# A grouped whitening kernel: partition rows reordered to (channel, sample), a round of 24 slots in place of 28, Gram pieces in halves and products of 392 columns

## The chip, the cores and the metric

One NeuronCore of one Trainium2 chip runs the whole kernel. The metric is the device time of one execution, in microseconds (us). Everything is float32.

## The reference

The input x is 32 samples by 128 channels by 56x56 pixels (3136). Four neighbouring channels of one sample are normalised together (group norm with 32 groups), and the result is whitened in 16 groups of 8 channels: the 8x8 covariance over all samples and pixels, its inverse square root, one product.

```python
def _gn(v, G=32, eps=1e-05):
    g = v.reshape(B_, G, C_ // G, H_, W_)
    m = jnp.mean(g, axis=(2, 3, 4), keepdims=True)
    s = jnp.var(g, axis=(2, 3, 4), keepdims=True)
    return ((g - m) / jnp.sqrt(s + eps)).reshape(v.shape)

def _zca_forward(x, weight, bias, groups=16):       # c = 8 channels, M = 32 * 3136
    xf = jnp.transpose(x, (1, 0, 2, 3)).reshape(C, M)
    xc = xf - jnp.mean(xf, axis=1, keepdims=True)
    xg = xc.reshape(G, c, M)
    cov = jnp.einsum('gim,gjm->gij', xg, xg) / M + 1e-4 * jnp.eye(c)
    e, v = jnp.linalg.eigh(cov)
    proj = jnp.einsum('gik,gk,gjk->gij', v, jax.lax.rsqrt(e), v)
    xw = jnp.einsum('gij,gjm->gim', proj, xg).reshape(C, M)
    return (xw * weight + bias)                     # back to (N, C, H, W)

x = x + _zca_forward(_gn(x), L0_conv_weight, L0_conv_bias)
```

## The kernel before

**Tiles.** A channel group (8 channels, g = 0 to 15) is two tiles, s = 0 and 1. A tile has 128 partition rows, 16 samples by 8 channels, and 3136 pixels in the free dimension: 1.6 MB. It is loaded into one of 13 places of `ring`, normalised in place, and overwritten with the output before it is stored. So 51.4 MB come in and 51.4 MB go out. In the kernel before, row p is sample p // 8, channel p % 8.

**What a group needs, in order.**
- Four loads per tile, each of 32 rows (4 samples by 8 channels), issued by GpSimd (`load`): `x_dram[g, s, q]`, with q = 0 and 2 in one pair and 1 and 3 in the next. They are issued two groups ahead of use.
- VectorE: 14 `row_stats` (448 columns each), then `stats_rows`, `stats_mean`, `stats_var`, `stats_reciprocal`, `stats_heron`, `stats_scale`, with two small averaging products on TensorE (`mean_average`, `var_average`) and a root on ScalarE between them. The last of them gives `y_mul` and `y_add`.
- GpSimd: `normalise`, 8 pieces of 784 columns, with the loads and small operations between them.
- VectorE: `turn`, 8 transposes in 32x32 blocks, of 13, 12, 12 and 12 units of 64 columns per tile, into a ring of three `y_t`. A turn needs the normalised columns that it covers; the first one of a tile covers 832 and so needs two pieces.
- TensorE: `gram`, one product of 64x64 per unit, added up in `ps_gram`. A float32 product is two MATMUL instructions, so a turn is 24 or 26 of them.
- VectorE: `gram_masked_blocks` and `gram_sum` read `ps_gram`; the first Gram product of the next group waits until the former has read it (`gram_masked`).
- The solve: 20 hops (`HOPS`), tiny products on TensorE, each of which needs what ScalarE or VectorE read of the one before: MU, COV, then 15 that alternate between two products read by ScalarE (`HOP_YUZ`) and one read by VectorE (`HOP_M`), then T, V and ROOT. VectorE makes of ROOT the 128x128 matrices `a_mat`, one for each tile.
- TensorE: `apply`, 14 products of 128x128 by 448 columns; ScalarE: `finish`, 8 evictions of two banks or one (896 or 448 columns) that add the shift and write the output into `ring`.
- SyncE: `store`, two DMAs per tile, of 64 rows each (8 samples by 8 channels), issued when the tile's last eviction is done. The last tile of all is stored in two parts.

**The order of the work.** It is written out by hand. Every engine runs the same loop over rounds i and over slots j of a round (`SLOTS`, 28). Each operation of a group has a slot number counted from the group's own round (`HOP_AT`, `APPLY_AT`, `TURN_AT`, `STAT_DVE_AT` and so on); a number of 28 or more falls into a later round. So in one round TensorE works on the Gram products of one group, on the solve of that group and the one before, and on the apply products of an older one, and VectorE gathers the statistics of the next group. Engines run strictly in their program's order, and semaphores make them wait for each other; within a slot TensorE's order is hop, averaging product, apply, Gram piece, and VectorE's is hop, `gram_masked_blocks`, turn, statistics, `row_stats`.

## Time and profile before

| | |
|---|---|
| time, median of 3 runs | 548.48 us (542.95 to 552.39) |
| time of the profiled execution | 546.78 us |
| its span, first to last instruction | 545.2 us |
| mean granted TensorE clock | 0.946 |
| TensorE busy | 420.7 us (77%) |
| VectorE busy | 318.2 us (58%) |
| GpSimd busy | 217.1 us (40%) |
| ScalarE busy | 154.3 us (28%) |
| DMA | 104.04 MB, mean 191 GB/s |

Busy shares are means over a span that has a start without products and an end without anything but stores, so they say little about which engine a round waits for. TensorE's small products overlap in the records: a product's modelled end lies up to 0.08 us behind the start of the next one. The profiled execution's time is its span and 1.6 us around it.

### The profile page before, as it was taken

How to read it: one execution, taken by the hardware profiler on the slowest of the kernel's cores; microseconds unless marked ns; L12 is line 12 of the kernel's file. 1: busy time of each engine (PE TensorE's matmuls, PEld its weight loads, DVE VectorE, ACT ScalarE, POOL GpSimd, SP SyncE). 2: the span in 40 equal slices, each digit the busy share in tenths (PEclk: the TensorE clock that was granted, in tenths of full speed). 3: DMA queues.
4: the chain of work that ended last, by engine and by line, in shares of the span. 5: the costliest groups of instructions: out<-in, count | busy, mean ns of one | idle time of the engine just before them, and what ended most of it. 6: DMA issues, size and time to landing. Idle time of an engine off the chain costs nothing.

```text
span 545.2 us, 11695 instructions
## 1 busy us (share of the span) xinstructions
PE 420.7 (77%) x4708; PEld 244.2 (45%) x4708; DVE 318.2 (58%) x853; ACT 154.3 (28%) x353; POOL 217.1 (40%) x324
## 2 busy tenths in 40 slices
PE   0036688888888989888988989898989888898820
PEld 0025554454455545444454545454554545553310
DVE  0668676767567676767576666766676766431100
ACT  0000013333233233332233323333333233333520
POOL 6054908172453627090815445361809060600000
PEclk9998569999899999999799999999999999999975
DMA  7965434757485857576575848485767634444443
GB/s 168 223 167 187 120 120 121 251 170 272 159 277 175 248 203 243 209 226 221 185 249 149 285 172 280 177 250 199 233 218 218 241 113 105 120 111 128 139 174 129
DMA packets 23652, 104.04 MB, mean 191 GB/s; under 512 B 15152, under 2 KB 15152, under 8 KB 15536
## 3 DMA queue, kind: packets, MB, share of 16 engines
q0 software_dynamic: 18432, 51.44, 30.6%
q1 hardware_dynamic: 5168, 51.87, 29.7%
q8 instruction: 38, 0.62, 0.5%
q14 instruction: 14, 0.11, 0.1%
HBM read 51.86 MB, written 51.38 MB: 189 GB/s over the span
## 4 chain that ended last, share of the span: by engine, by line
PE 55%; DMA 13%; DVE 11%; issue 7%; POOL 7%; ACT 3%; DVEq 0%; ACTq 0%; POOLq 0%
PE ps_apply L540 28%; DMA ring<-in_x_dram 13%; PE ps_gram L540 13%; PE ps_small L540 12%; POOL ring L294 3%; DVE bn L340 3%; POOL ring L288 3%; DVE y_t L389 3%; PE ps_stat L540 2%; ACT st L498 1%; DVE mv L346 1%; DVE a_mat L435 1%; DVE pp L417 1%; DVE pb L430 1%; ACT zx L498 1%
## 5 line engine op out<-in xcount | busy, mean ns | idle before, releaser
L294 POOL TENSOR_SCALAR ring<-ring,y_mul,y_add 128x784 f32<-128x784 f32 x128 | 126.6, 993 | 255.1 <-DVE y_add L379 253.4
L540 PE MATMUL ps_apply<-ring,a_mat 128*128 128x448 f32 x448 | 227.5, 594 | 0.6 <-ACT ring L492 0.3
L340 DVE BATCH_NORM_STATS2 bn<-ring 128x6 f32<-128x448 f32 x224 | 132.7, 598 | 22.5 <-DMA ring<-in_x_dram 22.4
L540 PEld LDWEIGHTS ps_gram<-y_t 128*64 128x64 f32 x3136 | 111.1, 146 | 59.8 <-issue 37.1
L492 ACT ACTIVATE ring<-ps_apply,fin_add 128x896 f32<-128x896 f32 (+1 forms) x128 | 115.7, 906 | 76.8 <-PE ps_apply L540 76.8
L540 PE MATMUL ps_gram<-y_t 128*64 128x64 f32 x3136 | 129.2, 235 | 8.9 <-DVE y_t L389 8.9
L389 DVE STREAM_TRANSPOSE y_t<-ring 128x768 f32<-128x768 f32 (+1 forms) x128 | 125.8, 984 | 16.1 <-POOL ring L294 16.1
L288 POOL DMA_DIRECT2D ring<-in_x_dram x128 | 75.9, 594 | 2.4 <-issue 1.4
L540 PEld LDWEIGHTS ps_apply<-ring,a_mat 128*128 128x128 f32 x448 | 68.6, 190 | 13.9 <-ACT ring L492 3.6
L417 DVE SCALAR_TENSOR_TENSOR pp<-ps_small,cst 16x16 f32<-16x16 f32 x112 | 17.5, 156 | 88.8 <-PE ps_small L540 88.2
L498 ACT COPY st<-ps_small 16x32 f32<-16x32 f32 (+1 forms) x128 | 22.2, 174 | 155.3 <-PE ps_small L540 155.3
L540 PEld LDWEIGHTS ps_small<-pp,st 16*16 16x16 f32 x224 | 12.4, 89 | 55.6 <-issue 53.5
L540 PE MATMUL ps_small<-st 16*16 16x16 f32 x224 | 23.0, 176 | 18.2 <-ACT st L498 18.2
L540 PEld LDWEIGHTS ps_small<-st 16*16 16x16 f32 x224 | 12.7, 89 | 44.4 <-issue 42.2
L540 PE MATMUL ps_small<-pp,st 16*16 16x16 f32 x224 | 23.2, 177 | 10.3 <-DVE pp L417 8.5
L540 PE MATMUL ps_small<-st,pp 16*16 16x16 f32 x256 | 25.2, 172 | 5.5 <-DVE pp L417 5.5
L540 PE MATMUL ps_stat<-mv,cst 128*128 128x2 f32 x32 | 6.5, 273 | 21.9 <-DVE mv L346 21.9
L540 PEld LDWEIGHTS ps_small<-st,pp 16*16 16x16 f32 x256 | 14.7, 89 | 6.7 <-issue 6.7
L540 PEld LDWEIGHTS ps_stat<-mv,cst 128*128 128x128 f32 x32 | 5.2, 203 | 24.2 <-DVE mv L346 13.9
L393 DVE TENSOR_TENSOR g_masked<-ps_gram,cst 128x64 f32<-128x64 f32 x16 | 3.6, 225 | 20.3 <-PE ps_gram L540 20.3
L498 ACT COPY mu<-ps_small 128x32 f32<-128x32 f32 x16 | 3.0, 186 | 43.0 <-PE ps_small L540 43.0
L498 ACT COPY zx<-ps_small 8x128 f32<-8x128 f32 x16 | 4.1, 255 | 36.1 <-DVE res L422 36.1
(59 smaller groups left out, 192.9 us busy)
## 6 DMA issues: line engine op xcount, KB each, us to landing
ring<-in_x_dram POOLq DMA_DIRECT2D x128, 392.0 KB, 8.2
out_dram<-ring SPq DMA_DIRECT2D x62, 784.0 KB
out_dram<-ring SPq DMA_DIRECT2D x2, 448.0 KB
out_dram<-ring SPq DMA_DIRECT2D x2, 336.0 KB
cst<-const_dram SPq DMA_DIRECT2D x1, 472.0 KB
wb<-in_L_conv_weight_dram SPq DMA_DIRECT2D x1, 0.5 KB
wb<-in_L_conv_bias_dram SPq DMA_DIRECT2D x1, 0.5 KB
```

What stands on the lines that cost most here:

```text
L288: pool.dma_start(ring[32 * q:32 * (q + 1), slot(g, s), :], x_dram[g, s, q]).then_inc(x_landed[slot(g, s)], 16)
L294: nc.gpsimd.tensor_scalar(y, y, y_mul[:, g, s:s + 1], y_add[:, g, s:s + 1], ALU.mult, ALU.add).then_inc(y_ready, 1)
L340: nc.vector.bn_stats(bn[:, g % 2, s, b, :], ring[:, slot(g, s), b * BN:(b + 1) * BN]).then_inc(bn_done, 1)
L346: nc.vector.bn_aggr(mv[:, g, s, :], bn[:, g % 2, s].rearrange("p b k -> p (b k)")).then_inc(stat_step, 1)
L389: nc.vector.transpose(y_t[:, n % TURN_RING, 0:hi - lo], ring[:, slot(g, s), lo:hi]).then_inc(turned, 1)
L393: nc.vector.tensor_tensor(g_masked[:], ps_gram[:, 0:UNIT], k_("gmask"), ALU.mult).then_inc(gram_masked, 1)
L417: nc.vector.scalar_tensor_tensor(out=pp[:], in0=s_m, scalar=POLY[it][1], in1=ai[:, 2 * CG * it:2 * CG * (it + 1)], op0=ALU.mult, op1=ALU.a ...
L430: nc.vector.tensor_tensor(by_sample(pb[:]), spread, by_sample(w_mask[:, g % 2]), ALU.mult).then_inc(tail_step, 1)
L435: nc.vector.scalar_tensor_tensor(out=a_mat[:, g % 2, s], in0=k_("ident"), scalar=scale[:, g, s:s + 1], in1=pb[:], op0=ALU.mult, op1=ALU.ad ...
L492: nc.scalar.activation(dst, ps_apply[:, bank:bank + chunks, 0:APPLY], ACT.Identity, bias=fin_add[:, g, s:s + 1], scale=1.0).then_inc(out_r ...
L498: nc.scalar.copy(dst, src).then_inc(solve_read, 1)
L540: return nc.tensor.matmul(out_, lhsT, rhs, start=start, stop=stop, skip_group_check=True)
```

## The change

- **Rows.** A tile's rows are now four bands of 32, and within a band row = channel * 4 + sample. The loads and the stores take their view of DRAM as (channel, sample) for each band: a load's outermost dimension is 8 channels where it was 4 samples; a store is four DMAs of 32 rows (8 channels by 4 samples) where it was two of 64 rows (8 samples by 8 channels). Masks and the views that spread a small matrix over samples follow (`by_sample`, `for_samples`), with one dimension more.
- **Slots.** A round has 24 slots where it had 28. The hops from the third on stand in successive slots (18 hops in 18 slots; before, 9 slots for 8 hops). A turn comes every third slot as before, its Gram products are split in two parts in the two slots that follow (6 units, then 6 or 7). The other slots take the apply products.
- **Products.** 16 apply products of 392 columns replace 14 of 448; each is evicted by itself (16 evictions of 392 columns where there were 8), two slots after it is issued, over four banks.
- **Statistics.** `row_stats` stand in two slots of three and end earlier; the averaging product of the mean is in slot 22 of the round before and that of the variance in slot 0; `stats_scale` is in slot 4 as before, the first turn in slot 6 where it was in slot 7.
- **Small.** The MU hop has one more product (a constant 128x128 by `neg_mean`, 2 columns), from which `fin_add` is made. Every tile is stored whole, the last too.

All the new names that depend on `BLOCKS` have their values for `BLOCKS = 1`: loops over it run once.

```diff
-APPLY = 448
-APPLY_TILE = HW // APPLY
-APPLY_CHUNKS = TILES * APPLY_TILE
-PIECE_CHUNKS = ((2, 2, 2, 1), (2, 2, 2, 1))
-PIECE_TILE = len(PIECE_CHUNKS[0])
-PIECES = TILES * PIECE_TILE
-CHUNK_PIECE = [(PIECE_TILE * s + k, b) for s in range(TILES) for k, n in enumerate(PIECE_CHUNKS[s]) for b in range(n)]
-PIECE_LAST = [max(c for c, (p, _) in enumerate(CHUNK_PIECE) if p == k) for k in range(PIECES)]
-SLOTS = 28
+BLOCKS = 1
+BLOCK = P // BLOCKS
+STRETCH = HW // BLOCKS
+APPLY = 392
+ROUND_TILE = STRETCH // APPLY
+ROUNDS = TILES * ROUND_TILE
+BANK_SETS = 4 // BLOCKS
+ROWS_OF = 4
+BANDS = P // (ROWS_OF * CG)
+STORED = 16 * BLOCKS * BANDS
+SLOTS = 24
...
-BN_AT = [2 * b for b in range(TILES * BN_CHUNKS)]
-STAT_DVE_AT = [28, 29, 30, 31, 31, 32]
-STAT_PE_AT = [28, 30]
-ROOT_AT = 31
-TURN_AT = [7 + 3 * b for b in range(TURNS)]
-GRAM_LAG = 2
-GRAM_READ_AT = TURN_AT[-1] + GRAM_LAG + 1
-HOP_AT = [GRAM_READ_AT, GRAM_READ_AT + 1] + [GRAM_READ_AT + 2 + (9 * k) // 8 for k in range(HOPS - 2)]
-APPLY_AT = [HOP_AT[-1] + 2 + 2 * c for c in range(APPLY_CHUNKS)]
-FINISH_LAG = 1
+BN_AT = [3 * (b // 2) + b % 2 + 1 for b in range(TILES * BN_CHUNKS)]
+STAT_DVE_AT = [BN_AT[-1] + 1 + k for k in (0, 2, 4, 6, 6, 7)]
+STAT_PE_AT = [BN_AT[-1] + 2, BN_AT[-1] + 4]
+ROOT_AT = BN_AT[-1] + 6
+TURN_AT = [6 + 3 * b for b in range(TURNS)]
+GRAM_AT = [a + 2 + h for a in TURN_AT for h in range(2)]
+GRAM_READ_AT = GRAM_AT[-1] + 1
+HOP_AT = [GRAM_READ_AT, GRAM_READ_AT + 2] + [GRAM_READ_AT + 3 + k for k in range(HOPS - 2)]
+FIRST_APPLY = next(a for a in range(HOP_AT[-1] + 2, HOP_AT[-1] + 5) if a % 3 == 1)
+APPLY_AT = [FIRST_APPLY + SLOTS * c // ROUNDS for c in range(ROUNDS)]
+FINISH_LAG = 2
...
-        x_dram = x.rearrange("(s q n) (g c) h w -> g s q n c (h w)", s=TILES, q=4, c=CG)
-        out_dram = out.rearrange("(s a n) (g c) h w -> g s a n c (h w)", s=TILES, a=2, c=CG)
+        x_dram = x.rearrange("(s q n) (g c) h w -> g s q c n (h w)", s=TILES, q=BANDS, c=CG)
+        out_dram = out.rearrange("(s q n) (g c) h w -> g s q c n (h w)", s=TILES, q=BANDS, c=CG)
...
         def by_sample(a):
-            return a.rearrange("p (n c) -> p n c", c=CG)
+            return a.rearrange("p (q c n) -> p q c n", c=CG, n=ROWS_OF)
+        def for_samples(a):
+            return a.unsqueeze(1).unsqueeze(3).broadcast_to([P, BLOCK // (ROWS_OF * CG), CG, ROWS_OF])
...
         def _(sp):
             def store(g, s, lo, hi):
-                px = slice(lo, hi)
-                for a in range(2):
-                    rows = slice(a * HALF, (a + 1) * HALF)
-                    sp.dma_start(out_dram[g, s, a, :, :, px],
-                                 ring[rows, slot(g, s), px]).then_inc(out_stored[slot(g, s)], 16)
+                for r in range(BLOCKS):
+                    for q in range(BANDS):
+                        k, band = divmod(q, BANDS // BLOCKS)
+                        px = slice(k * STRETCH + lo * APPLY, k * STRETCH + hi * APPLY)
+                        at = slice(r * STRETCH + lo * APPLY, r * STRETCH + hi * APPLY)
+                        sp.dma_start(out_dram[g, s, r * (BANDS // BLOCKS) + band, :, :, px],
+                                     ring[32 * q:32 * (q + 1), slot(g, s), at]).then_inc(out_stored[slot(g, s)], 16)
             sp.dma_start(cst[:], const).then_inc(const_landed, 16)
             with nc.allow_non_contiguous_dma(reason="256 channel scalars, once"):
                 sp.dma_start(wb8[:, 0, :], weight.rearrange("(g j) o -> j (g o)", j=CG)).then_inc(const_landed, 16)
...
-            for g in range(GROUPS - 1):
-                for s in range(TILES):
-                    sp.wait_ge(out_ready, PIECES * g + PIECE_TILE * (s + 1))
-                    store(g, s, 0, HW)
-            g = GROUPS - 1
-            sp.wait_ge(out_ready, PIECES * g + PIECE_TILE)
-            store(g, 0, 0, HW)
-            sp.wait_ge(out_ready, PIECES * g + PIECE_TILE + 2)
-            store(g, 1, 0, 4 * APPLY)
-            sp.wait_ge(out_ready, PIECES * (g + 1))
-            store(g, 1, 4 * APPLY, HW)
+            for n in range(TILES * GROUPS):
+                g, s = divmod(n, TILES)
+                sp.wait_ge(out_ready, BLOCKS * ROUND_TILE * (n + 1))
+                store(g, s, 0, ROUND_TILE)
             for n in range(TILES * GROUPS - RING, TILES * GROUPS):
-                extra = 32 if n == TILES * GROUPS - 1 else 0
-                sp.wait_ge(out_stored[n % RING], 32 * (n // RING + 1) + extra)
+                sp.wait_ge(out_stored[n % RING], STORED * (n // RING + 1))
...
-                nc.vector.tensor_reduce(g_pad[:, CG:2 * CG], g_masked[:].rearrange("p (n c) -> p c n", c=CG),
-                                        AX.X, ALU.add).then_inc(gram_reduced, 1)
+                nc.vector.tensor_reduce(g_pad[:, CG:2 * CG], g_masked[:].rearrange("p (q c n) -> p c q n", c=CG, n=ROWS_OF),
+                                        AX.XY, ALU.add).then_inc(gram_reduced, 1)
...
-            def finish(g, k):
-                s, b = divmod(k, PIECE_TILE)
-                if k == 0:
+            def finish(g, c):
+                s, h = divmod(c, ROUND_TILE)
+                n = ROUNDS * g + c
+                if c == 0:
                     act.wait_ge(shift_step, 2 * (g + 1))
-                chunks = PIECE_CHUNKS[s][b]
-                hi = (PIECE_LAST[k] + 1 - APPLY_TILE * s) * APPLY
-                act.wait_ge(applied, APPLY_CHUNKS * g + PIECE_LAST[k] + 1)
-                dst = ring[:, slot(g, s), hi - chunks * APPLY:hi].rearrange("p (b c) -> p b c", c=APPLY)
-                bank = 2 * (k % 2)
-                nc.scalar.activation(dst, ps_apply[:, bank:bank + chunks, 0:APPLY], ACT.Identity,
-                                     bias=fin_add[:, g, s:s + 1], scale=1.0).then_inc(out_ready, 1)
+                act.wait_ge(applied, n + 1)
+                for r in range(BLOCKS):
+                    at = r * STRETCH + h * APPLY
+                    nc.scalar.activation(ring[:, slot(g, s), at:at + APPLY],
+                                         ps_apply[:, BLOCKS * (n % BANK_SETS) + r, 0:APPLY], ACT.Identity,
+                                         bias=fin_add[:, g % 2, r, s:s + 1], scale=1.0).then_inc(out_ready, 1)
...
-                        act.wait_ge(tail_step, TAIL_OPS * g)
-                    copy(mu[:], s_mu)
+                        act.wait_ge(shift_step, 2 * g)
+                    copy(mu[:], ps_small[:, 0:32 + TILES * BLOCKS])
...
-                nc.scalar.activation(fin_add[:, g], neg_mean[:, g], ACT.Identity, bias=shift[:],
-                                     scale=-1.0).then_inc(shift_step, 1)
+                nc.scalar.activation(fin_add[:, g % 2].rearrange("p r s -> p (r s)"), mu[:, 4 * CG:], ACT.Identity,
+                                     bias=shift[:], scale=-1.0).then_inc(shift_step, 1)
...
-            def gram(g, t):
+            def gram(g, k):
+                t, part = divmod(k, 2)
                 b = t % TURN_TILE
                 n = TURNS * g + t
-                pe.wait_ge(turned, n + 1)
-                if t == 0 and g > 0:
+                if part == 0:
+                    pe.wait_ge(turned, n + 1)
+                if k == 0 and g > 0:
                     pe.wait_ge(gram_masked, g)
-                for u in range(TURN_UNITS[b]):
+                for u in range(6 * part, TURN_UNITS[b] if part else 6):
                     half = ps_gram[UNIT * (u % 2):UNIT * (u % 2 + 1), 0:UNIT]
                     unit = y_t[:, n % TURN_RING, u * UNIT:(u + 1) * UNIT]
                     ins = product(half, unit, unit, start=t == 0 and u < 2,
                                   stop=t == TURNS - 1 and u >= TURN_UNITS[b] - 2)
-                ins.then_inc(gram_done, 1)
+                if part == 1:
+                    ins.then_inc(gram_done, 1)
             def apply(g, c):
-                s, b = divmod(c, APPLY_TILE)
-                k, place = CHUNK_PIECE[c]
+                s, h = divmod(c, ROUND_TILE)
+                n = ROUNDS * g + c
                 if c == 0:
                     wait_apart(pe, tail_step, TAIL_OPS * g + 4)
-                n = PIECES * g + k
-                if place == 0 and n >= 2:
-                    pe.wait_ge(out_ready, n - 1)
-                product(ps_apply[:, 2 * (k % 2) + place, 0:APPLY], a_mat[:, g % 2, s],
-                        ring[:, slot(g, s), b * APPLY:(b + 1) * APPLY]).then_inc(applied, 1)
+                if n >= BANK_SETS:
+                    pe.wait_ge(out_ready, BLOCKS * (n - BANK_SETS + 1))
+                for k in range(BLOCKS):
+                    for r in range(BLOCKS):
+                        rows, at = slice(r * BLOCK, (r + 1) * BLOCK), k * STRETCH + h * APPLY
+                        ins = product(ps_apply[k * BLOCK:(k + 1) * BLOCK, BLOCKS * (n % BANK_SETS) + r, 0:APPLY],
+                                      a_mat[rows, g % 2, s], ring[rows, slot(g, s), at:at + APPLY])
+                ins.then_inc(applied, 1)
...
+                    for r in range(BLOCKS):
+                        product(s_dup[:, r * TILES:(r + 1) * TILES], k_("dup")[:, r * P:(r + 1) * P], neg_mean[:, g])
...
-                    for t, back in due([a + GRAM_LAG for a in TURN_AT], j):
+                    for t, back in due(GRAM_AT, j):
```

Worked out from the new lists, the slots of a round hold on TensorE, in this order (a hop by its number of the 20): slot 7 hop 0 (MU), apply; 8 apply, Gram; 9 hop 1 (COV), Gram; 10 hop 2, apply; 11 hop 3, apply, Gram; 12 hop 4, Gram; 13 hop 5, apply; 14 hop 6, apply, Gram; 15 hop 7, Gram; and so on in threes to slot 21 hop 13, Gram; 22 hop 14, mean product, apply; 23 hop 15, apply, Gram; 0 hop 16, variance product, Gram; 1 hop 17 (T), apply; 2 hop 18 (V), apply, Gram; 3 hop 19 (ROOT), Gram; 4 apply; 5 apply, Gram; 6 Gram.

## Rows read from the trace of the kernel before

**Rows 1.** Windows of rounds: start:end, length, busy (instructions), clock, DMA share, GB/s.
```profile
172.69:201.62 28.93, 25.35 (x296) 14.46 (x295) 19.80 (x54) 9.55 (x22) 13.55 (x21) 1.00 0.68 222
112.69:143.75 31.06, 27.11 (x296) 15.26 (x295) 19.87 (x54) 9.54 (x22) 13.56 (x20) 0.95 0.65 220
260.41:291.89 31.48, 28.00 (x296) 15.79 (x295) 19.93 (x54) 9.55 (x22) 13.56 (x21) 0.89 0.64 202
```

**Rows 2.** Timeline of GpSimd: first normalisation of groups 0, 2 and 15 (start, duration).
```profile
33.12 0.99 POOL L294 TENSOR_SCALAR ring<-ring,y_mul,y_add 128x784 f32<-128x784 f32 x1 [22.47 <-DVE y_add L379]
...
83.73 0.99 POOL L294 TENSOR_SCALAR ring<-ring,y_mul,y_add 128x784 f32<-128x784 f32 x1 [14.60 <-DVE y_add L379]
...
465.90 1.00 POOL L294 TENSOR_SCALAR ring<-ring,y_mul,y_add 128x784 f32<-128x784 f32 x1 [19.97 <-DVE y_add L379]
```

**Rows 3.** Timeline of TensorE in one round; brackets: idle before, and its releaser.
```profile
200.66 1.02 PE L540 MATMUL ps_apply<-ring,a_mat 128*128 128x448 f32 x2
201.61 0.21 PE L540 MATMUL ps_small<-pp,st 16*16 16x16 f32 x2
...
202.23 0.20 PE L540 MATMUL ps_small<-st 16*16 16x16 f32 x2 [0.35 <-ACT st L498]
...
209.08 0.92 PE L540 MATMUL ps_gram<-y_t 128*64 128x64 f32 x24
209.93 0.21 PE L540 MATMUL ps_small<-pp,st 16*16 16x16 f32 x2
...
220.35 0.38 PE L540 MATMUL ps_small<-res,zx 8*128 8x8 f32 x2 [0.53 <-ACT zx L498]
...
225.14 0.38 PE L540 MATMUL ps_stat<-mv,cst 128*128 128x2 f32 x2 [0.81 <-DVE mv L346]
225.38 1.00 PE L540 MATMUL ps_apply<-ring,a_mat 128*128 128x448 f32 x2
```

**Rows 4.** Timeline of VectorE: steps around the solve's last hop and the turns.
```profile
31.89 0.15 DVE L366 RECIPROCAL rec<-root 128x2 f32<-128x2 f32 x1
...
115.01 1.05 DVE L389 STREAM_TRANSPOSE y_t<-ring 128x832 f32<-128x832 f32 x1 [0.77 <-POOL ring L294]
...
220.77 0.29 DVE L430 TENSOR_TENSOR pb<-ps_small,w_mask 128x128 f32<-128x128 f32 x1 [0.76 <-PE ps_small L540]
...
221.77 0.62 DVE L340 BATCH_NORM_STATS2 bn<-ring 128x6 f32<-128x448 f32 x1
...
223.70 0.96 DVE L389 STREAM_TRANSPOSE y_t<-ring 128x768 f32<-128x768 f32 x1
224.58 0.51 DVE L346 BATCH_NORM_AGGREGATE mv<-bn 128x2 f32<-128x42 f32 x2
...
228.40 0.23 DVE L393 TENSOR_TENSOR g_masked<-ps_gram,cst 128x64 f32<-128x64 f32 x1 [1.02 <-PE ps_gram L540]
```

**Rows 5.** Timeline of VectorE: waits for loads.
```profile
29.54 0.63 DVE L340 BATCH_NORM_STATS2 bn<-ring 128x6 f32<-128x448 f32 x1 [2.77 <-DMA ring<-in_x_dram]
...
136.76 0.63 DVE L340 BATCH_NORM_STATS2 bn<-ring 128x6 f32<-128x448 f32 x1 [0.60 <-DMA ring<-in_x_dram]
```

**Rows 6.** Timeline of TensorE: its wait behind the second of these.
```profile
137.88 0.38 PE L540 MATMUL ps_stat<-var,cst 128*128 128x2 f32 x2 [0.42 <-DVE var L354]
```

**Rows 7.** Timeline of ScalarE: the last two evictions of the kernel.
```profile
520.65 1.53 ACT L492 ACTIVATE ring<-ps_apply,fin_add 128x896 f32<-128x896 f32 x2 [0.50 <-PE ps_apply L540]
```

**Rows 8.** Windows: loads alone twice, the fastest microsecond, stores alone twice.
```profile
6.50:34.00 27.50, 2.57 (x8) 2.00 (x8) 12.29 (x35) 0.20 (x1) 5.03 (x9) 1.00 1.01 226
39.00:40.00 1.00, 1.00 (x24) 1.00 (x20) 1.00 (x3) 0.00 (x0) 1.00 (x3) 1.00 0.53 201
213.00:214.00 1.00, 0.65 (x8) 0.35 (x7) 0.56 (x2) 0.00 (x0) 1.00 (x2) 1.00 0.94 389
486.00:500.00 14.00, 12.19 (x126) 6.65 (x126) 3.43 (x14) 5.43 (x12) 0.00 (x0) 1.00 0.42 112
524.00:540.00 16.00, 0.00 (x0) 0.00 (x0) 0.00 (x0) 0.00 (x0) 0.00 (x0) 0.50 0.48 188
```

56 lines of the change are left out of this document (30 added, 26 removed).

## The prediction

> **What bounds the kernel now.** I read the windows of whole rounds first [rows 1]. From the first normalisation of one group to that of the next an ordinary round takes 28.93 us; TensorE is recorded busy for 25.35 of it, VectorE for 19.8, GpSimd 13.55, ScalarE 9.55. So a round is TensorE's program plus its waits. The timeline of GpSimd [rows 2] cuts the span of 545.2 us in four: 33.1 us until group 0 is normalised for the first time; 50.6 us for the first two rounds, which hold few or no apply products; 382.2 us for 13 full rounds (13 x 28.93 would be 376.1, so 6.1 us are extra); 79.3 us after the last group's start.
>
> TensorE's timeline [rows 3] says what the waits are: a hop of the solve that comes behind nothing but its predecessor. The two products at 201.61 are short, yet the next hop starts 0.62 us later, for ScalarE's read and the semaphores; where a Gram piece or an apply product lies between, there is no wait. A round holds seven such waits of 0.35 to 0.53 us and one of 0.81 for `stats_rows` [rows 3]. The recorded idle time is 28.93 - 25.35 = 3.6 us; each wait is really some 0.08 us longer, because a product's recorded end lies behind the start of the next (200.66 + 1.02 against 201.61). With eight waits that is 4.2 us, and 24.7 us of work.
>
> The extra 6.1 us sit mainly in two rounds of 31.06 and 31.48 us, whose granted clock was 0.95 and 0.89 [rows 1]: in each the clock fell from 2.4 to 1.2 GHz. The first fall came after TensorE had waited 0.81 us for the mean and then 0.42 us behind VectorE [rows 6], which itself waited for a load [rows 5]. A round with a fall cost 2.1 and 2.5 us, some 0.5 of the first being the wait.
>
> The ends are bound by DMA. VectorE waits for the third tile until 29.54 [rows 5] and group 0 starts 3.6 us later. The last eviction ends at 522.2 [rows 7], the span 23.0 us after it; in between only stores run [rows 8].
>
> **The change: work of a round.** An apply product of 448 columns takes 0.95 us start to start (200.66 to 201.61), a product of 2 columns 0.24 (225.14 to 225.38) [rows 3]; on that line one of 392 takes 0.86. Sixteen are 13.8 us for 13.3: +0.5 (bounds: 0, if time goes with the columns, and +1.9, if it goes with the instructions). MU's added product is of 2 columns: +0.24. The Gram instructions are the same (24 in 0.85 us); halving them adds eight seams, taken at nothing, up to +0.5. So 24.7 + 0.7 = 25.4 us. The evictions are 16 of 392 columns; ScalarE rises from 9.55 to about 11.5 us of the round, hidden, because four banks give each eviction some four slots.
>
> **The change: waits of a round.** With a hop in each slot every hop from the third to T, V and ROOT has at least half a Gram piece (0.42 us) behind it, and its own issue, some 0.12 for a product (0.20 less the overlap of 0.08) and more for two. That is 0.54 to 0.61 against the 0.62 that passed between 201.61 and 202.23: the seven waits go, but for less than 0.1 each, which I take at nothing. What is late next I follow in VectorE's program, which is strictly in order. Let T be the start of hop ROOT.
> - VectorE reads ROOT at T + 0.42 and is free at T + 1.42 (220.35, 220.77, 221.77) [rows 3, 4]. Then stands the eighth turn (0.88, from 223.70 to 224.58), then `stats_reciprocal`, from which to GpSimd's first piece 1.23 us pass (31.89 to 33.12) [rows 2, 4]: T + 3.5. The first turn needs two pieces, 2.3 us after GpSimd's start (112.69 to 115.01) [rows 1, 4], and takes 0.97; behind it on VectorE stands `gram_masked_blocks` (0.23), for which the first Gram piece waits: T + 7.1.  TensorE needs only 0.32 + 0.42 + 1.72 (two apply) + 0.85 + 0.53 (MU with its new product) + 1.72 = 5.6 us to get there. A new wait of 1.5 us in every round; behind it in TensorE's order stand COV and so the whole solve.
> - VectorE reads COV only behind two `row_stats`: 0.3 us.
> - `stats_rows` stands in slot 21 behind hop 13's read and a turn: it is done 0.24 + 0.1 + 0.88 + 0.56 = 1.8 us after that hop's start; TensorE is there after 0.13 + 0.54 + 0.19. A wait of 0.9, like the 0.81 that it has now [rows 3].
>
> Together 2.7 us, and the round is 25.4 + 2.7 = 28.1, 0.8 less than 28.93. A seventh fewer slots thus gives only 3% of a round: the hops' waits are gone, one of VectorE's and GpSimd's chain has come.
>
> **The change: the clock.** TensorE stands 1.5 us in one place of every round, with the small products of COV behind it, where the 1.23 us (0.81 + 0.42) before the first fall came in two parts. None of the rounds with 0.81 alone had a fall. I therefore expect a fall in some eight of 13 rounds, between none and all, at 2.0 us (the two observed, less the wait in the first): +16.
>
> **The change: transfers.** One pair of loads alone moved 201 GB/s with a DMA share of 0.53: half of the 16 engines, four for each DMA, as many as its outermost dimension (4 samples) [rows 8]. Stores, whose outermost dimension is 8, run at 0.42 and 0.48. With all loads queued in the opening the share is 1.01 and the rate only 226 GB/s: 14 GB/s for each engine, which elsewhere moves 24. So something other than the engines is shared; in one microsecond 389 GB/s were reached. Stores alone likewise run at 112 GB/s and at 188 with the same share. The new layout gives every DMA 8 channels outermost and 32 rows, 4 for each of 8 engines. No row shows a DMA of the new shape. I take 330 GB/s for the opening (bounds 226, no gain, and 389; nearer to the latter, since a pair alone already gives each engine its full 24) and 190 for stores (the 188 without company; bounds 112 and half of 389 at 0.94, which is 207).
>
> The Trainium skill, page SBUF — State Buffer, section Door 1: The DMA port swizzle, says that partitions reach 16 ports in blocks of four and that 0 to 31 and 32 to 63 share eight of them. 
>
> In us: three tiles (4.8 MB) at 330 land by 6.5 + 14.6 = 21.1 for 29.5; VectorE's statistics are then the later, and group 0 starts at about 25: -8 (bounds 0 and -9.5). At the end the last two tiles are evicted 6 us apart; each is stored in 8.5 us at 190 GB/s, so the last, now whole, has its data out 11 us after the last eviction, and with 2 for latency and SyncE's issues the span ends 13 after it, for 23.0: -10 (at 112 GB/s it would be +2). In the rounds no load is late any more.
>
> **The sum**, on the profiled execution's 546.8: opening -8; first two rounds, four slots shorter each and with fewer bare hops, -5 (estimate, 0 to -7); 13 rounds 13 x 28.1 = 365.3 for 382.2, -16.9; clock +16; from the last group's start to the last eviction 56.3 us now, slot 4 to slot 79 in place of 80, but with an emptier TensorE and 16 products: +3 (estimate, 0 to +5); stores -10. That gives 525.9. The median of the runs is 0.3% above the profiled one, within what I can tell: 526.
>
> **The rivals.**
> - *The clock holds.* All as above, falls as rare as now (two, 4 us): 514; with none 510. For it: TensorE's work before the wait is dense, two apply products. Against: [rows 6]. Chance 0.25.
> - *It falls in every round*, once: 13 x 2.0 = +26: 536, and 540 if each costs the larger 2.5. Chance 0.13.
> - *The transfers gain nothing*, because what is shared is not touched by the layout: opening 0, stores 0, and some 2 us of load waits as now: 526 + 20 = 546, no change. Chance 0.12.
> - *Slower: two falls in every round.* Place: the wait of 1.5 us and the wait of 0.9 for `stats_rows`, some 14 us apart, so that the clock returns and falls again. Price: 26 x 2.0 = +52 for +16: 562; it ends above 546.8 from 1.4 falls a round. Against: the wait of 0.81 alone brought none now [rows 1, 3]. Chance 0.05.
> - My forecast, falls in about half to three quarters of the rounds and freer transfers: 518 to 533. Chance 0.45.
>
> **How the numbers follow.** Something like 2% (11 us, 537.5) is what the runs tell from no change. Range 507 to 543: it takes in the forecast, the clock that holds, one fall in every round, and most of what the bounds of the product's cost give (-7 and +18 over 13 rounds); the transfers that gain nothing and the slower rival stay outside. Faster by over 2%: 0.45 + 0.25 + 0.08 = 0.78; within: 0.12 + 0.05 = 0.17; slower: 0.05.
>
> **What would show it.** Starts of GpSimd's first pieces 28 us apart, 30 where the window's clock is below 1; TensorE waiting about 1.5 us at the first Gram piece of each group and 0.9 at the mean's product, and no more 0.35 behind hops; group 0 normalised at about 25 us; DMA share near 1 with over 300 GB/s in the opening; about 12 us from the last eviction to the end. The prediction is wrong if the first Gram piece waits markedly less (then the round is nearer 27) or more, if the 392-column product takes over 0.9 us, if the opening stays at 226 GB/s, or if the clock behaves otherwise.

## The result and the profile after

The changed kernel takes 594.08 us (median of 4 runs, 586.21 to 597.17) against 547.75 us before in the same session: ratio 1.079, 95% interval 1.060 to 1.099. It is 8% slower, where 526 us was forecast. The profiled execution took 592.77 us with a span of 591.0. (Ratios here leave disturbed runs out.)

GpSimd's timeline of the changed kernel, first normalisation of groups 0, 2 and 15, answers to [rows 2]:

```profile
24.43 0.99 POOL L302 TENSOR_SCALAR ring<-ring,y_mul,y_add 128x784 f32<-128x784 f32 x1 [14.37 <-DVE y_add L387]
...
69.84 0.99 POOL L302 TENSOR_SCALAR ring<-ring,y_mul,y_add 128x784 f32<-128x784 f32 x1 [13.30 <-DVE y_add L387]
...
509.83 0.99 POOL L302 TENSOR_SCALAR ring<-ring,y_mul,y_add 128x784 f32<-128x784 f32 x1 [24.99 <-DVE y_add L387]
```

ScalarE's timeline, the last evictions, answers to [rows 7]; the last ends at 574.15:

```profile
562.76 11.39 ACT L499 ACTIVATE ring<-ps_apply,fin_add 128x392 f32<-128x392 f32 x19
```

These rows cut the time as the prediction cut it:

| part of the span, us | before | forecast | after |
|---|---|---|---|
| until group 0 is normalised | 33.1 | 25.1 | 24.4 |
| first two rounds | 50.6 | 45.6 | 45.4 |
| 13 full rounds | 382.2 | 365.3 + 16 | 440.0 |
| last group's start to the last eviction | 56.3 | 59.3 | 64.3 |
| last eviction to the end | 23.0 | 13.0 | 16.8 |

Of the 67 us between forecast and result, 59 lie in the 13 rounds. Below, a *fall* is a stretch in which the granted clock is 1.2 in place of 2.4 GHz. Windows of the changed kernel (columns as in [rows 1]): a round, the fall in it, the stretch from its end to the next fall, then the opening and the stores at the end, which answer to [rows 8]:

```profile
239.60:273.74 34.14, 30.34 (x300) 17.51 (x300) 21.00 (x54) 10.53 (x30) 13.21 (x21) 0.85 0.51 188
242.60:252.84 10.24, 9.22 (x52) 4.41 (x53) 5.07 (x9) 2.44 (x7) 7.67 (x12) 0.50 0.88 303
252.84:276.73 23.89, 21.12 (x252) 13.10 (x252) 15.92 (x45) 8.10 (x23) 5.54 (x9) 1.00 0.36 140
8.00:20.00 12.00, 0.79 (x2) 0.50 (x2) 8.49 (x21) 0.00 (x0) 2.06 (x4) 1.00 1.02 425
577.00:591.00 14.00, 0.00 (x0) 0.00 (x0) 0.00 (x0) 0.00 (x0) 0.00 (x0) 0.50 0.41 175
```

From 106 us on every round holds one fall, 13 in all, each 10.24 us long. The page's row of the clock, in 40 slices of 14.8 us, shows them as a beat:

```profile
PEclk9999999697997969798796969889696978979995
```

Where TensorE stands still is told by its chain of waits (total us, times, longest), and the timeline of one round shows what is behind the waits:

```profile
PE ps_gram L548 <- DVE g_masked L401: 24.3, 14, 2.1
PE ps_stat L548 <- DVE mv L354: 19.3, 16, 7.2
PE ps_small L548 <- DVE pp L420: 15.2, 15, 1.2
```

```profile
273.47 1.05 DVE L397 STREAM_TRANSPOSE y_t<-ring 128x832 f32<-128x832 f32 x1 [1.46 <-POOL ring L302]
274.43 0.18 DVE L401 TENSOR_TENSOR g_masked<-ps_gram,cst 128x64 f32<-128x64 f32 x1
...
274.77 0.57 PE L548 MATMUL ps_gram<-y_t 128*64 128x64 f32 x12 [1.72 <-DVE g_masked L401]
...
275.91 0.98 POOL L302 TENSOR_SCALAR ring<-ring,y_mul,y_add 128x784 f32<-128x784 f32 x1
276.02 0.16 DVE L415 SCALAR_TENSOR_TENSOR st<-ps_small,cst 16x16 f32<-16x16 f32 x1
...
276.21 1.43 DVE L420 SCALAR_TENSOR_TENSOR pp<-st,cst 16x16 f32<-16x16 f32 x1
276.87 0.40 POOL L322 TENSOR_TENSOR w_mask<-cst,w_rows 128x128 f32<-128x128 f32 x1
...
277.79 0.21 PE L548 MATMUL ps_small<-pp,st 16*16 16x16 f32 x2 [1.20 <-DVE pp L420]
```

The first wait is the forecast one: VectorE's turn waits for two of GpSimd's pieces and `gram_masked_blocks` stands behind it. The second is new. L420 works on 16x16 elements and takes 1.43 us; in the kernel before the same instruction (L412) took 0.16 at every group, in the round of [rows 1] at 172.03, before GpSimd's first piece at 172.69. Here GpSimd is busy at that time, normalising and weighing the mask, and L420 is through some 0.4 us after `w_mask`, at 277.6. All of this line's instructions, first in the kernel before, then in the changed one (ns, least/median/longest):

```profile
L412 DVE SCALAR_TENSOR_TENSOR pp<-st,cst x16: 161/162/164, 54.8 to 492.8; 16x16 f32<-16x16 f32 x16
```

```profile
L420 DVE SCALAR_TENSOR_TENSOR pp<-st,cst x16: 161/1426/1433, 48.7 to 545.1; 16x16 f32<-16x16 f32 x16
```

The short one, 161 ns, is the last, at 545.1 us, when GpSimd has no work left.

TensorE's timeline gives its prices at both levels of the clock. At half clock an apply product takes 1.60 us start to start (283.41 to 285.01), at full clock 0.86 (288.21 to 289.07), and half a Gram piece 0.50 (290.06 to 290.56):

```profile
283.41 1.68 PE L548 MATMUL ps_apply<-ring,a_mat 128*128 128x392 f32 x2
285.01 0.23 PE L548 MATMUL ps_small<-pp,st 16*16 16x16 f32 x2
...
288.21 0.93 PE L548 MATMUL ps_apply<-ring,a_mat 128*128 128x392 f32 x2
289.07 0.21 PE L548 MATMUL ps_small<-st 16*16 16x16 f32 x2
...
290.06 0.57 PE L548 MATMUL ps_gram<-y_t 128*64 128x64 f32 x12
290.56 0.21 PE L548 MATMUL ps_small<-pp,st 16*16 16x16 f32 x2
```

### The profile page after: what moved, and what is told of

Read it like the earlier page. It is cut to its first block, busy times and chain, and to the rows that moved or that the text cites. A ratio compares the mean times of both kernels' runs of the same rounds, so it can differ in the third digit from the quotient of the medians.

```text
span 591.0 us, 12077 instructions
## 1 busy us (share of the span) xinstructions
PE 489.3 (83%) x4804; PEld 291.3 (49%) x4804; DVE 332.8 (56%) x853; ACT 171.1 (29%) x481; POOL 211.9 (36%) x324
## 3 DMA queue, kind: packets, MB, share of 16 engines
q0 software_dynamic: 10240, 51.40, 25.1%
## 4 chain that ended last, share of the span: by engine, by line
PE 65%; DVE 18%; POOL 6%; issue 6%; DMA 1%; ACT 0%; DVEq 0%; POOLq 0%
PE ps_apply L548 35%; PE ps_gram L548 17%; PE ps_small L548 11%; DVE y_t L397 6%; POOL ring L302 5%; DVE pp L420 3%; DVE bn L348 2%; PE ps_stat L548 2%; DVE mv L354 1%; DMA ring<-in_x_dram 1%; DVE a_mat L443 1%; DVE scale L379 1%; DVE pb L438 1%; DVE y_mul L385 0%; DVE y_add L387 0%
## 5 line engine op out<-in xcount | busy, mean ns | idle before, releaser
L548 PE MATMUL ps_apply<-ring,a_mat 128*128 128x392 f32 x512 | 264.7, 618 | 0.2 <-ACT ring L499 0.2
L548 PE MATMUL ps_gram<-y_t 128*64 128x64 f32 x3136 | 165.8, 252 | 33.7 <-DVE g_masked L401 24.3
L548 PEld LDWEIGHTS ps_gram<-y_t 128*64 128x64 f32 x3136 | 131.5, 158 | 117.6 <-issue 60.4
L499 ACT ACTIVATE ring<-ps_apply,fin_add 128x392 f32<-128x392 f32 x256 | 142.2, 574 | 3.1 <-PE ps_apply L548 1.3
L348 DVE BATCH_NORM_STATS2 bn<-ring 128x6 f32<-128x448 f32 x224 | 129.2, 602 | 11.4 <-DMA ring<-in_x_dram 11.4
L548 PEld LDWEIGHTS ps_apply<-ring,a_mat 128*128 128x128 f32 x512 | 91.1, 214 | 23.4 <-issue 4.2
L296 POOL DMA_DIRECT2D ring<-in_x_dram x128 | 71.7, 569 | 1.0 <-POOLq L658 0.9
L548 PE MATMUL ps_small<-pp,st 16*16 16x16 f32 x224 | 24.1, 182 | 16.7 <-DVE pp L420 15.2
L420 DVE SCALAR_TENSOR_TENSOR pp<-st,cst 16x16 f32<-16x16 f32 x16 | 18.7, 1170 | 0.0
L430 DVE SCALAR_TENSOR_TENSOR res<-ps_small,cst 8x8 f32<-8x8 f32 x16 | 2.5, 154 | 21.5 <-PE ps_small L548 21.5
L524 ACT ACTIVATE shift<-pmu,wb 128x1 f32<-128x1 f32 x16 | 6.2, 387 | 28.2 <-DVE pmu L446 28.2
```

Of the source, the lines that this page charges most:

```text
L296: pool.dma_start(ring[32 * q:32 * (q + 1), slot(g, s), :], x_dram[g, s, q]).then_inc(x_landed[slot(g, s)], 16)
L348: nc.vector.bn_stats(bn[:, g % 2, s, b, :], ring[:, slot(g, s), b * BN:(b + 1) * BN]).then_inc(bn_done, 1)
L420: nc.vector.scalar_tensor_tensor(out=pp[:], in0=blocks, scalar=POLY[0][1], in1=ai[:, 0:2 * CG], op0=ALU.mult, op1=ALU.add).then_inc(solve_ ...
L499: nc.scalar.activation(ring[:, slot(g, s), at:at + APPLY], ps_apply[:, BLOCKS * (n % BANK_SETS) + r, 0:APPLY], ACT.Identity, bias=fin_add[ ...
L524: nc.scalar.activation(shift[:], pmu[:], ACT.Identity, bias=wb[:, 1, g:g + 1], scale=wb[:, 0, g:g + 1]).then_inc(shift_step, 1)
L548: return nc.tensor.matmul(out_, lhsT, rhs, start=start, stop=stop, skip_group_check=True)
```

## The experiments

Each edits the changed kernel if nothing else is said. "Falls" are those between 100 us and the last eviction, out of some 14 groups' rounds; an undisturbed round is one without a fall. Falls are counted in one trace of each kernel, and its other executions can differ: with the same program e1 took 542.62 to 607.45 us, e4 513.08 to 529.41. A small difference in the number of falls between two kernels is therefore no evidence by itself.

**One wait at a time.** e1 computes `pp` from PSUM and one constant, no longer from `st` and a constant, both in SBUF; the constant `first_pp` holds `POLY[0][0] + POLY[0][1] * ZCA_EPS / TRACE` on its diagonal. VectorE's wait for ScalarE's copy goes too; it cost nothing, L420 started right behind L415 (276.21 for 276.02 + 0.16):

```
-                    dve.wait_ge(cov_copied, g + 1)
-                    nc.vector.scalar_tensor_tensor(out=pp[:], in0=blocks, scalar=POLY[0][1], in1=ai[:, 0:2 * CG],
+                    nc.vector.scalar_tensor_tensor(out=pp[:], in0=s_first, scalar=POLY[0][1] * 0.5 / TRACE,
+                                                   in1=k_("first_pp", 2 * CG),
```

> pp is computed from PSUM (s_first) and one SBUF constant, in place of st and ai, which are both in SBUF; nothing else changes. Theory A (the port: the instruction of 16x16 with two SBUF inputs takes 1170 ns because it cannot proceed beside GpSimd's normalise): L420 falls to about 0.16 us, the wait of 1.20 us before the first YUZ products falls to 0.1, and if the clock still falls once a round, the round goes from 34.1 to about 33.1 and the time from 594 to about 579. Theory B (the instruction is slow for another reason, such as reading what was just written): L420 stays above 0.5 us and the time within 1% of 594. Theory C (the wait at this place, 2.5 us behind the first one, is what tips the clock): falls in fewer than half of the rounds and a time of 520 to 540.

Measured: 549.28 us (10 runs, 542.62 to 607.45), ratio to before 0.996 (0.990 to 1.003). L420 takes 0.15 us while GpSimd still normalises:

```profile
L420 DVE SCALAR_TENSOR_TENSOR pp<-ps_small,cst x16: 151/152/153, 48.2 to 505.2; 16x16 f32<-16x16 f32 x16
```

Theory A holds on the instruction and B is refuted: what was slow was the second SBUF input beside GpSimd's work. Reading the `st` that was just written is not it, for the changed kernel's last L420 does so too and took 161 ns, with GpSimd idle. The Trainium skill, page SBUF — State Buffer, section Who interferes with whom, states just this case: a VectorE instruction with two SBUF inputs contends with a GpSimd instruction that reads SBUF, one with at most one, outside VectorE's 2-port modes, does not. Both halves agree with 1.43 and 0.15 us here. Of the time, 45 us are gone, 17 by the wait's length (15 x 1.15); the rest goes with the falls, nine in place of 13, four of them 3.4 us long. That is neither A's 579 nor C's 520 to 540. The windows of an undisturbed round and of one with such a fall:

```profile
160.00:189.00 29.00, 26.37 (x301) 15.88 (x302) 19.65 (x54) 10.55 (x30) 13.27 (x20) 1.00 0.61 223
383.10:413.70 30.60, 27.97 (x301) 16.39 (x302) 19.71 (x54) 10.55 (x30) 13.29 (x20) 0.94 0.56 211
```

e2 reorders the turns, so that the first needs one normalise piece:

```
-TURN_UNITS = (13, 12, 12, 12)
+TURN_UNITS = (12, 12, 12, 13)
```

> TURN_UNITS (12, 12, 12, 13): the first turn of a tile takes 768 columns and so needs one normalise piece of 784 instead of two. Theory A (the wait of 1.72 us at the first Gram piece is VectorE's and GpSimd's chain): the first turn starts 1.15 us earlier, the wait falls to about 0.6, and with a fall of the clock still in every round the round is about 33.0 and the time 577. Theory C (the length of this wait is what brings the fall): falls in fewer than half of the rounds, 515 to 540. Rival (the 10.2 us at half clock set the round, whatever the waits around them): round stays at 34.1, time 594.

Measured: 586.81 us, ratio to before 1.062 (1.047 to 1.077), 12 falls, most of 13.7 us. The wait behind `g_masked` went from 24.3 to 2.7 us in all, and only 7 us of time came of it: longer falls ate the rest. That misses the numbers of theories A and C; the mean of its 13 rounds, 33.95 us, is near the rival's 34.1. The falls have also moved: seven of the eight of 13.7 us begin 1.3 to 1.5 us behind the start of the mean's product, for which TensorE waited 0.97 us. In the changed kernel all 13 begin 1.9 to 2.4 us behind that of the first Gram piece.

e11 moves `stats_rows` to the head of its slot on VectorE, ahead of the hop's read and the turn:

```
                 for j in range(SLOTS):
+                    if j == STAT_DVE_AT[0] % SLOTS and in_step(0, i + 1):
+                        stats_rows(i + 1)
...
-                            (stats_rows, stats_mean, stats_var, stats_reciprocal, stats_heron,
+                            (lambda g: None, stats_mean, stats_var, stats_reciprocal, stats_heron,
```

> The changed kernel with stats_rows alone moved to the head of its slot on VectorE; pp and the turns as in the changed kernel. If only this wait's length is saved and a fall comes in every round as before: 34.1 - 0.9 = 33.2 us, time about 581. If all that counts is how much TensorE stands still in a round: some falls go, 560 to 575. If the falls come from the two waits around the first Gram piece alone: 13 falls remain.

Measured: 578.69 us, ratio 1.055 (1.047 to 1.064), 12 falls of 3.4 to 20.5 us. That is near the 581 expected from the length alone, 0.9 a round; the falls are nearly as many as in the changed kernel, of other lengths.

**Two and three waits.** e4 is e1 with e2, e12 is e1 with e11, e9 has all three.

> The edits of the first two together, no fill. If the falls stay in every round: 34.1 - 1.1 - 1.1 = 31.9 us a round, time about 562. If the two waits together are what lets the clock fall (theory C): falls in few rounds, 27.5 to 28.5 us a round, time 505 to 520.

> The changed kernel with pp from PSUM and stats_rows at the head of its slot; turns of (13, 12, 12, 12), so that the wait of 1.7 us at the first Gram piece stays and is the only long one. Undisturbed round 29.05 - 0.9 = 28.15 us. If a fall needs two waits close together (first Gram piece and pp): no falls behind the opening, time about 515. If the wait of 1.7 us with the small products of COV behind it is enough: falls of 3.4 us and more in at least half of the rounds, 530 to 545.

> All three waits of the changed kernel's round taken away at their source: pp from PSUM, turns of (12, 12, 12, 13), and stats_rows at the head of its slot on VectorE instead of behind a hop's read and a turn. With the first two the undisturbed round was 27.97 us. Theory A (TensorE's standing still is what brings the falls, and each wait counts its length in the round): the wait of 0.97 at the mean's product goes, round 27.1 us, no fall behind the opening, time 500 to 515. Rival (another chain, VectorE's from hop ROOT to the first normalisation, sets the round next): round stays above 27.7, time 515 to 528.

Measured: e4 528.61 us (513.08 to 529.41) with two falls in the rounds and one of 51.2 us in the opening, which makes the round from group 2 to group 3 39.2 us long, so that the median meets neither of its two expectations; e12 522.42 us, ratio 0.951 (0.939 to 0.964); e9 494.80 us (493.22 to 495.26), ratio 0.903 (0.897 to 0.908). Windows of undisturbed rounds of e4, of e12 (behind a round with a fall) and of e9:

```profile
217.40:245.30 27.90, 26.41 (x301) 15.89 (x300) 19.59 (x54) 10.55 (x30) 13.25 (x20) 1.00 0.61 233
```

```profile
182.90:212.60 29.70, 27.93 (x302) 16.43 (x302) 19.88 (x54) 10.53 (x30) 13.26 (x21) 0.94 0.59 219
298.40:326.50 28.10, 26.33 (x301) 15.92 (x302) 19.80 (x54) 10.53 (x30) 13.25 (x20) 1.00 0.62 230
```

```profile
256.10:283.00 26.90, 26.39 (x302) 15.94 (x300) 19.75 (x54) 10.53 (x30) 13.22 (x20) 1.00 0.64 237
```

| kernel | waits left: first Gram, pp, mean (us) | undisturbed round | falls | median, us |
|---|---|---|---|---|
| changed | 1.72, 1.20, 0.86 | 30.2 (own, and e14) | 13 | 594.1 |
| e2 | about 0.5, 1.1, 0.97 | - | 12 | 586.8 |
| e11 | 1.72, 1.20, - | - | 12 | 578.7 |
| e1 | 1.72, -, 0.86 | 29.05 | 9 | 549.3 |
| e4 | about 0.5, -, 0.97 | 27.97 | 2 | 528.6 |
| e12 | 1.72, -, - | 28.12 | 6 of 3.4 us | 522.4 |
| e9 | about 0.4, -, - | 26.92 | 0 | 494.8 |

The undisturbed round loses each wait's length, 1.15, 1.1 and about 1.0. The falls get fewer as waits are taken away, and not in proportion: e2 and e11, with one wait gone, lose one fall each. In e12, where the first Gram piece's wait is the only long one, it is followed by a fall in six rounds: theory "two waits are needed" is refuted, and the other's 530 to 545 misses too, since all six last only 3.4 us. e9 stays below its 500 to 515, with 0.2 less a round and no fall in the rounds; the rival of another chain is refuted.

**Work in place of waiting.** If standing still brings the falls, products whose result nobody reads must cure them. e3 puts two ahead of the first Gram piece, into the free eighth bank:

```
+                if k == 0:
+                    for _ in range(2):
+                        product(ps_fill[:, 0:448], k_("ones"), cst[:, 0:448])
                 if part == 0:
                     pe.wait_ge(turned, n + 1)
```

> Two products of 448 columns of constants into a spare PSUM bank, without any reader, stand ahead of the first Gram piece of each group, where TensorE waits; they add work and compute nothing. Theory A (it is TensorE's standing still there that brings the fall of the clock, and the fall costs some 4.7 us of every round): the granted clock stays at 1.00 in most rounds, rounds of 29.5 to 30 us, time 525 to 540. Theory B (the round is set by VectorE's and GpSimd's chain and the half clock lies beside it): time within 1% of 594 though the clock is higher. Theory D (the fall comes from the small products of COV and the wait behind them, which this does not fill): falls stay, time 594 to 605.

Measured: 561.83 us, ratio 1.025 (1.016 to 1.033); two falls in place of 13. Adding 32 products took 32 us away. VectorE's and GpSimd's work is unchanged, so theory B, that the half clock lies beside a chain of theirs, is refuted. Above the expected 540 it stays because the two falls last 20.5 us and a third, in the opening, 27.3. The two begin within 0.2 us of the end of TensorE's wait of 1.21 us for `pp`, which this fill leaves. Windows that hold an undisturbed round, and one with a fall (223.7 to 262.5, 38.8 us):

```profile
292.80:323.20 30.40, 28.06 (x306) 16.79 (x306) 21.10 (x54) 10.55 (x30) 13.34 (x21) 1.00 0.57 212
222.00:262.50 40.50, 38.11 (x332) 21.43 (x331) 22.63 (x60) 12.02 (x34) 13.29 (x20) 0.75 0.44 160
```

e7 adds one such product to e4 at the same place; e13 adds it to e4 ahead of the mean's product instead.

> pp from PSUM, turns of (12, 12, 12, 13), and one product of 448 columns of constants into a spare bank ahead of the first Gram piece of each group. Without it the undisturbed round was 27.97 us with 0.7 us of waiting there. Theory A (a fall comes from TensorE standing still): no fall behind the opening, round 28.2 to 28.4, time 512 to 520. Rival (the falls that are left come from elsewhere, such as the wait for the mean's product): falls as often as without the fill, each round 0.3 longer: 530 to 535.

> pp from PSUM, turns of (12, 12, 12, 13), and one product of 448 columns of constants ahead of the mean's product, where TensorE otherwise waits 0.97 us for stats_rows; the product computes nothing. The undisturbed round was 27.97 us without it and stays within 0.1 of that, since it only fills the wait. Theory A (the falls that were left, and the additional ones with a fill at the first Gram piece, come from TensorE standing still at the mean's product): no fall behind the opening, time 508 to 518. Rival (the falls come from somewhere else): three to seven falls behind the opening, 525 to 550.

Measured: e7 547.64 us (534.75 to 554.11) with six falls of 13.7, e13 511.40 us, ratio 0.949 (0.937 to 0.960), with none and a round of 27.96. e7 refutes its theory A as written: less standing still at one place gave more falls than in e4, and every execution of e7 was slower than every one of e4. Its trace shows all six elsewhere, 1.4 to 1.6 us behind the start of the mean's product (the first of them begins at 124.8):

```profile
123.45 0.38 PE L551 MATMUL ps_stat<-mv,cst 128*128 128x2 f32 x2 [0.97 <-DVE mv L357]
```

and e13, which fills just that wait, has none and is faster than e7 in every execution. Against e4 its gain is less sure: the fastest execution of e4, 513.08, lies within e13's 507.98 to 518.18. So 0.97 us there can bring a fall or not; in e4's trace it did twice, in e7's six times. What decides between the two was not found.

e14 puts one ahead of the first YUZ products only, e15 has that and e3's two.

> The changed kernel with one product of 448 columns of constants ahead of the first YUZ products, where TensorE waits for pp. If the standing still inside the half-clock phase is what prolongs the falls to 10.2 us: they shorten to 3.4, round 34.1 - 2.9 = 31.3, time about 550. If it is the two waits together that bring the fall: they vanish in most rounds, 530. If neither (only the wait at the first Gram piece counts): falls and time as in the changed kernel, 590 to 597.

> The changed kernel with two such products ahead of the first Gram piece and one ahead of the first YUZ products. With the first two alone the undisturbed round was 30.32 us, with two falls of 20.5 us in the rounds and 562 us. Theory A: no fall behind the opening, round 30.3, time 545. Rival (as many falls as with the first two alone, as they start near the mean's product): 560.

Measured: e14 563.18 us, ratio 1.046 (1.039 to 1.053), ten falls, six of 3.4, two of 6.8 and two of 10.2 us; e15 551.08 us (ratio 1.015, 0.986 to 1.043), one fall of 13.7 in the rounds. Filling the wait for pp alone changed the falls' length more than their number: the standing still inside the half-clock stretch (TensorE waits until 243.62 in the one from 242.60) is the likely reason for the length; it prolongs the fall in most rounds, not in all. That the number changed little fits the changed kernel's trace, where the falls begin 0.3 to 1.1 us before this wait ends. e15 fills both: the two falls of e3 are gone, and its one fall begins 1.5 us behind the start of the mean's product, the wait that is left. It comes between its theory's 545 with none and its rival's 560. e14 also shows the changed kernel's own round undisturbed, its three waits in it:

```profile
135.40:165.60 30.20, 27.42 (x303) 16.24 (x303) 20.87 (x54) 10.53 (x30) 13.21 (x20) 1.00 0.58 215
```

**The parts of the change alone.** e5 is the kernel before with the new rows, e6 the changed kernel with the old ones. The core of e5's diff (masks, averages and `by_sample` go with it as in the changed kernel):

```
-x.rearrange("(s q n) (g c) h w -> g s q n c (h w)", s=TILES, q=4, c=CG)
+x.rearrange("(s q n) (g c) h w -> g s q c n (h w)", s=TILES, q=BANDS, c=CG)
...
-                for a in range(2):
+                for q in range(BANDS):
```

> The kernel before with the new rows alone: partitions of a band of 32 as (channel, sample), masks and averages to match, loads of 8 channels outermost, four stores of 32 rows for a tile; order of the work, product of 448 columns and split of the last store as before. Theory A (the transfers gain what the changed kernel's trace shows at its ends: first normalisation 24.4 for 33.1, tail some 6 us shorter): 533 to 537 us, ratio 0.97 to 0.98. Rival (the gain at the ends is lost to something in the rounds, such as doubled issues on SyncE or strides of the masks): 545 to 550, ratio 1.00.

> The changed kernel with the old rows: (sample, channel), two stores of 64 rows. Theory A (the new order of the work, not the layout, brings the 8%): rounds of 34.1 with a fall of the clock in each, ends as before, time 605 to 615. Rival (the loads of the new layout collide with something and bring the stalls): rounds shorter than 33, time below 590.

Measured: e5 526.23 us, ratio 0.953 (0.948 to 0.959); e6 596.91 us, ratio 1.082 (1.073 to 1.091). In e5 the first normalisation starts at 23.46 (9.7 us earlier), the last eviction ends at 512.4 and the span 14.2 later (8.8 less), and the rounds are those of before, 28.90 us, with two falls; in all it is faster than the 533 to 537 that its theory A gave. An undisturbed round and one with a fall:

```profile
219.90:248.80 28.90, 25.36 (x296) 14.46 (x295) 19.78 (x54) 9.53 (x22) 13.21 (x20) 1.00 0.62 224
248.80:280.20 31.40, 27.96 (x295) 15.79 (x294) 19.86 (x54) 9.53 (x22) 13.22 (x20) 0.89 0.58 205
```

So the rows are worth 4.7% and the order of the work costs all of the 8% and more. e6 misses its 605 to 615: in the new order the rows are worth some 3 us (the two intervals of the ratio overlap), not 25. Its opening is 5 us later than the changed kernel's, but its 13 rounds average 33.3 us against 33.8, with falls of 3.4 and 6.8 us among them; the last eviction is followed by 22.4 us for 16.8. The two parts don't add: what the rows gain at the ends, the falls take in the rounds.

e8 is e4 with whole Gram pieces, in the first of their two slots.

```
-                for u in range(6 * part, TURN_UNITS[b] if part else 6):
+                if part == 1:
+                    return
+                for u in range(TURN_UNITS[b]):
```

> pp from PSUM and turns of (12, 12, 12, 13), with each Gram piece whole in the first of its two slots, as in the kernel before. Theory A (the split pays: it covers ScalarE's and VectorE's reads of the hops): the seam of 0.15 us for each of eight pieces goes, -1.2 us a round, but waits of some 0.35 come back behind four to six hops, +1.4 to +2.1, and TensorE stands still more often: round 28.0 to 29, time 525 to 540. Rival (the split costs its seams and covers little): round 27 us, time 515.

Measured: 550.56 us, ratio 1.002 (0.998 to 1.005), undisturbed round 29.7 against 27.97, seven falls of 3.4 us and one of 13.7, and more time than either theory said. The bare hops are back in its waits:

```profile
PE ps_small L549 <- ACT st L507: 12.8, 36, 0.4
PE ps_small L549 <- DVE pp L426: 11.8, 34, 0.3
```

The split does what it is for: with its seams it is worth 1.8 us of a round.

**The opening.** e9 has one fall left, from 36.2 to 70.3 us, in the rounds that have no apply products. e10 puts a product of 392 columns into every second of their slots. The loop over rounds and slots gives 18 of them, and the trace holds their 36 MATMULs; the 23 of the expectation was miscounted.

```
                         if in_step(0, i - back):
                             apply(i - back, c)
+                        elif i >= 0 and i - back < 0 and c % 2 == 0:
+                            product(ps_fill[:, 0:APPLY], k_("ones"), cst[:, 0:APPLY])
```

> The same, with a product of 392 columns of constants into a spare bank in every second slot that holds apply products later, for the rounds in which there is no apply product yet (23 products, which compute nothing). Theory A (the long fall of the clock in the opening, which makes the fourth round 39 instead of 28 us, comes from TensorE's idle first rounds): no fall before 100 us, at least 8 us less than without: 492 to 507. Rival (the first rounds are too empty to be filled by 23 products): within 1% of the kernel without them.

Measured: 488.39 us (6 runs, 488.20 to 488.61), ratio to before 0.891 (0.887 to 0.896), the fastest kernel of this study. The same stretch in e9 and in e10:

```profile
36.20:70.30 34.10, 30.20 (x360) 24.71 (x362) 27.08 (x76) 3.74 (x17) 19.16 (x32) 0.50 0.43 138
```

```profile
36.20:70.30 34.10, 32.45 (x451) 21.43 (x449) 30.13 (x84) 4.97 (x22) 21.77 (x36) 1.00 0.49 159
```

TensorE gets 91 more instructions done in the same time, 20 of them those of the added products. It brought 6.4 us, which is neither the expected 8 nor within 1%. In the two traces the spans differ by 6.2: 4.9 until group 3 is normalised, and 1.6 behind the last eviction (15.2 us for 16.8), where nothing was changed. And the clock is not shown to be the cause: two of e9's six executions had a mean clock of 0.988, like e10's (0.988 and 0.989), and so no such fall in the opening, and still took 494.99 and 493.22 us. What else the added products change was not found.

## Why the prediction was wrong

Two steps failed: an instruction's time taken from rows where GpSimd was idle, and the length of the clock's falls, which set their price. The sum's terms, in the order of the prediction:

- **Opening -8, first two rounds -5**: right (24.4 for 25.1, 45.4 for 45.6). The opening moved 425 GB/s for an assumed 330; as forecast, VectorE's statistics became the later and took what more there was. All these loads are of 32 rows, so the doubt that smaller DMAs gain nothing is answered. Why the rate rose is not shown: bands 0 and 1 stand on the same partitions as before, so the ports that the prediction has them share are shared still, and the change also halved the packets under 512 B, from 15152 to 7456. No run separates the two.
- **The hops' waits go**: right; behind ScalarE's `st` TensorE waited five times in the whole kernel, and e8 shows them come back.
- **The price of the seams, "taken at nothing, up to +0.5"**: too small even at its bound. Half a Gram piece takes 0.50 us, not 0.42, and eight pieces make +1.2. e9's round, with some 0.4 us of waiting, has 26.5 us of work for the forecast 25.4.
- **"VectorE reads COV only behind two row_stats: 0.3 us"**: the first step that failed. I followed VectorE's order but took its durations from rows where GpSimd was idle. The new slots put L420 beside GpSimd's normalise; it takes 1.43 us and the wait is 1.20. By its length that is +0.9 a round, but e1 shows it worth 45 us with the falls that hang on it.
- **The waits of 1.5 and 0.9**: right (1.72 and 0.86; the steps up to T + 7.1 add up to 7.0), and e2, e4 and e9 confirm both mechanisms.
- Together the undisturbed round is 30.2 us for 28.1, and longer than the 28.93 of before: +27 us over 13 rounds.
- **The clock, "some eight of 13 rounds at 2.0 us", +16**: the second step that failed. The 13 rounds hold 12 falls and average 33.85 us, 13 x (33.85 - 30.2) = +47. The rival of a fall in every round was named with 0.13, at 536 to 540 (at 2.5 each its sum is 542). What failed most is the price: 2.0 came from falls of 3.4 and 6.8 us in the kernel before. Here they last 10.24 and each costs 3.9. Per us at half clock the cost is alike, 0.38 here, 0.45 in e12 (29.65 - 28.12 for 3.4 us): the length was mis-sized, not the slowing. That the wait of 1.72 us comes first was seen rightly: all 13 falls follow it.
- **Last start to last eviction +3**: +8, of which one fall of 10.2 us (515.7) makes some 4.
- **Stores -10**: -6. The stores ran at 175 GB/s for 190. e5, which keeps the split of the last tile's store, has 14.2 us behind the last eviction for the changed kernel's 16.8; but of the runs that store it whole ten have 15.2 there and three 16.8, so the split may be worth no more than 1 us. What makes the two lengths was not found.

So 27.3 (longer undisturbed round) + 31.4 (falls) + 5.0 (last group) + 3.8 (stores) - 0.9 (opening and first rounds) make the 67 us. The sign was wrong because both terms of the rounds failed the same way; the layout's gain was forecast at 20 and measured alone at 25 (551.2 to 526.2 in medians; the profiled spans differ by 18.6).

What stays open: what makes a fall last 10.2 us in one kernel and 3.4 in another, and when a wait of 1 us brings one. Standing still is shown as the cause of most falls (e3, e9, and e13 against e7), the rule of it is not. It needs no long wait each time: the second fall of the kernel before (261.2) and both of e5's have only bare hops' waits of at most 0.4 us in the 3 us before them.

## What to carry to other kernels

When a schedule is rewritten, look for each moved VectorE instruction with two SBUF inputs what GpSimd does at its new time: a duration from the old trace is that of the old neighbours. Price a wait of TensorE of about a microsecond at its length plus the fall of the clock that can follow it, here some 0.4 of the stretch at half clock, and read that stretch's length from more than one trace. When one wait is taken away, look behind the next one: in e2 the falls moved there. Remove such waits at their source first, which here turned a loss of 8% into a gain of 10%, and try products into a spare bank where a wait can't be removed: e3 gained by it, e7 lost, and e13, with the same product at another wait, did not.
